# Graph attention kernel: one-hot rows of an edge tile made once for two node tiles, ring of ten, first head's K blocks copied by ScalarE

## What is computed

```python
q = (x @ Wq + bq).reshape(n, H, OUT_DIM); k = ...; v = ...
alpha = jnp.einsum('ehc,ehc->eh', q[dst], k[src]) / np.sqrt(OUT_DIM)
amax = jax.ops.segment_max(alpha, dst, num_segments=n)
ex = jnp.exp(alpha - amax[dst])
denom = jax.ops.segment_sum(ex, dst, num_segments=n)
attn = ex / denom[dst]
agg = jax.ops.segment_sum(attn[:, :, None] * v[src], dst, num_segments=n).reshape(n, HC)
x_attn = agg + x @ Wskip + bskip
h = x_attn @ Wlin + blin + x_attn[:, :OUT_DIM]      # then a layer norm, and x + ...
```

## Time and profile before

| | us |
|---|---|
| median of 3 runs | 1163.88 (1163.66 to 1164.5) |
| the profiled execution, its own time | 1169.78 |
| its span, first to last instruction | 1167.9 |
| TensorE matmuls busy | 1090.4 (93%) |
| VectorE busy | 583.9 (50%) |
| ScalarE busy | 323.4 (28%) |
| GpSimd busy | 125.5 (11%) |

### The profile page before, as it was taken

The page is one execution under the profiler, slowest core; times in us unless marked ns, Lnnn a source line. Parts: engine busy times, 40 slices in busy tenths (PEclk is TensorE's granted clock), DMA queues, the critical chain, the costliest instruction groups (busy, mean ns, idle before and its releaser), DMA issues.

```text
span 1167.9 us, 14839 instructions
## 1 busy us (share of the span) xinstructions
PE 1090.4 (93%) x5666; PEld 892.3 (76%) x5666; DVE 583.9 (50%) x1563; ACT 323.4 (28%) x492; POOL 125.5 (11%) x282
## 2 busy tenths in 40 slices
PE   5789999999999999999999999999999999989871
PEld 4676666668888888888888888888888888868650
DVE  4778888744343343324343332433333245676777
ACT  3443334211232322123232121322322133233210
POOL 1201010100000000000000000000000002535464
PEclk9899999989999999999999999999999999999885
DMA  9426364330010010002000100100010010000111
GB/s 296 177 90 210 122 228 161 120 145 1 1 72 1 1 47 27 2 1 72 1 1 15 58 2 1 73 1 1 1 72 1 1 37 10 18 18 19 36 36 35
DMA packets 14206, 64.42 MB, mean 55 GB/s; under 512 B 1939, under 2 KB 2332, under 8 KB 10553
## 3 DMA queue, kind: packets, MB, share of 16 engines
q1 hardware_dynamic: 9529, 46.67, 11.7%
q0 software_dynamic: 4608, 16.78, 3.7%
HBM read 44.11 MB, written 19.34 MB: 54 GB/s over the span
## 4 chain that ended last, share of the span: by engine, by line
PE 67%; DVE 18%; issue 7%; ACT 4%; POOL 2%; DMA 1%; POOLq 0%; DVEq 0%; SPq 0%; ACTq 0%
PE ps_o L1084 7%; PE ps_o L1086 7%; PE ps_o L1085 7%; PE ps_r L1084 7%; PE ps_r L1086 6%; PE ps_r L1085 6%; PE ps_s L1086 5%; PE ps_s L1085 5%; PE ps_s L1084 5%; PE ps_t L1291 3%; DVE opnd_lo L684 3%; PE ps_t L1084 2%; DVE onehot_src L695 2%; PE ps_t L1086 1%; PE ps_t L1085 1%
## 5 line engine op out<-in xcount | busy, mean ns | idle before, releaser
L1084 PE MATMUL ps_s<-xT_hi,tT 128*128 128x512 f32 (+1 forms) x480 | 176.2, 367 | 2.0 <-DVE top L1041 2.0
L1085 PE MATMUL ps_s<-xT_lo,tT 128*128 128x512 f32 (+1 forms) x480 | 171.2, 357 | 0.0
L1086 PE MATMUL ps_s<-xT_hi,tT 128*128 128x512 f32 (+1 forms) x480 | 171.1, 356 | 0.0
L1084 PE MATMUL ps_o<-y,pT 128*128 128x512 f32 x400 | 158.6, 397 | 0.0
L1086 PE MATMUL ps_o<-y,pT 128*128 128x512 f32 x400 | 157.5, 394 | 0.0
L1085 PE MATMUL ps_o<-y,pT 128*128 128x512 f32 x400 | 157.3, 393 | 0.0
L649 ACT ACTIVATE prob<-prob,nbias 125x1250 f32<-125x1250 f32 x40 | 53.7, 1342 | 259.4 <-DVE nbias L1049 259.4
L1041 DVE CUSTOM_DVE_ANT_0 prob<-ps_s,maskb 125x1250 f32<-125x1250 f32 x40 | 58.2, 1456 | 120.5 <-issue 120.5
L907 DVE TENSOR_TENSOR pT<-ps_t,pT 128x500 fp32r<-128x500 f32 (+1 forms) x120 | 67.3, 589 | 94.0 <-ACT pT L604 94.0
L604 ACT ACTIVATE pT<-ps_t 128x500 fp32r<-128x500 f32 (+1 forms) x120 | 57.9, 518 | 202.2 <-PE ps_t L1291 202.2
L1084 PEld LDWEIGHTS ps_s<-xT_hi,tT 128*128 128x128 f32 (+1 forms) x480 | 90.9, 189 | 18.1 <-DVE top L1041 2.5
(11 more groups left out here) (244 smaller groups left out, 1971.7 us busy)
## 6 DMA issues: line engine op xcount, KB each, us to landing
products<-prod_parts POOLq DMA_DIRECT2D x32, 512.0 KB, 3.2
gbuf<-products SPq DMA_DIRECT2D x4, 2048.0 KB, 7.8
mbuf<-products SPq DMA_DIRECT2D x4, 2048.0 KB, 7.9
stage<-in_Wq SPq DMA_DIRECT2D x4, 1024.0 KB, 7.0
stage<-in_Wk SPq DMA_DIRECT2D x4, 1024.0 KB, 5.2
stage<-in_Wskip SPq DMA_DIRECT2D x4, 1024.0 KB, 5.4
stage<-in_Wv SPq DMA_DIRECT2D x3, 1024.0 KB, 4.8
stage<-in_Wlin SPq DMA_DIRECT2D x3, 1024.0 KB, 4.7
```

The costliest lines, as they stand in the source:

```text
L1084: nc.tensor.matmul(out_, a[0], b[0], start=start, stop=False)
L1085: nc.tensor.matmul(out_, a[0], b[1], start=False, stop=False)
L1086: return nc.tensor.matmul(out_, a[1], b[0], start=False, stop=stop)
```

## The change

Each edge tile's pair of rows is made once, in the product of the first window that holds the tile (`tiles_begun(d)`: 18, then 16 in each, then 14), and used by each window that holds it. The buffer is t modulo 10, and the wait before it is for the last use of tile t - 10. `onehot_dst` is made 250 wide for the 36 tiles that two windows share, and the second window reads columns 125 to 249. VectorE makes the new tiles of a window in quarters of four (`quarter(tiles_begun(p - 1), i)`), TensorE still uses a window in quarters of five. The K blocks of head 0 are copied into `acc` by ScalarE, in its place for block copies, and no longer by VectorE. Three tiles are laid over others to make room (`at_plane`, `spill`, the fallback's row).

```diff
-RING = 9
+RING = 10
-def part(d, i):
-
-    w = window(d)
-    return w[len(w) * i // KC:len(w) * (i + 1) // KC]
+def quarter(some, i):
+
+    return some[len(some) * i // KC:len(some) * (i + 1) // KC]
+def tiles_begun(d):
+
+    return [t for t in window(d) if d == 0 or t not in window(d - 1)]
+def windows_of(t):
+
+    return [d for d in range(NT) if t in window(d)]
+def uses_before(d, t):
+
+    return sum(len(window(e)) for e in range(d)) + len([u for u in window(d) if u < t])
...
-        onehot_dst = [put(f"onehot_dst{i}", [P, R], BF16) for i in range(RING)]
+        onehot_dst = [put(f"onehot_dst{i}", [P, 2 * R], BF16) for i in range(RING)]
...
                 h, kind = divmod(p, 3)
                 if kind == K_PROD:
+                    if h == 0:
+                        act.wait_ge(prod_done, 4 * p + i + 1)
+                        nc.scalar.activation(acc[:, i, :], wbank[i], ACT.Copy).then_inc(prod_free, 1)
...
-            def onehots(d, some):
+            def onehots(some):
                 for t in some:
-                    i = made[0]
-                    if i >= RING:
-                        dve.wait_ge(onehot_used, i - RING + 1)
-                    nc.vector.tensor_scalar(onehot_src[i % RING][0:R, 0:NP], node_id[0:R, 0:NP],
+                    i = t % RING
+                    if t >= RING:
+                        last = windows_of(t - RING)[-1]
+                        dve.wait_ge(onehot_used, uses_before(last, t - RING) + 1)
+                    nc.vector.tensor_scalar(onehot_src[i][0:R, 0:NP], node_id[0:R, 0:NP],
                                             edge_p[0:R, 0, t:t + 1], edge_p[0:R, 1, t:t + 1],
                                             ALU.is_equal, ALU.mult)
-                    nc.vector.tensor_scalar(onehot_dst[i % RING][0:R, :], node_id[0:R, R * d:R * d + R],
-                                            edge_f[0:R, 1, t:t + 1], None, ALU.is_equal).then_inc(onehot_ready, 1)
-                    made[0] += 1
+                    a, w = R * windows_of(t)[0], R * len(windows_of(t))
+                    nc.vector.tensor_scalar(onehot_dst[i][0:R, 0:w], node_id[0:R, a:a + w],
+                                            edge_f[0:R, 1, t:t + 1], None,
+                                            ALU.is_equal).then_inc(onehot_ready, 1)
...
                 for i in some:
+                    if kind == K_PROD and h == 0:
+                        continue
                     dve.wait_ge(prod_done, 4 * p + i + 1)
                     if kind == K_PROD:
                         a = acc[:, i, :]
-                        if h == 0:
-                            ins = nc.vector.tensor_copy(a, wbank[i])
-                        else:
-                            ins = nc.vector.tensor_tensor(a, wbank[i], a, ALU.add)
-                        ins.then_inc(prod_free, 1)
+                        nc.vector.tensor_tensor(a, wbank[i], a, ALU.add).then_inc(prod_free, 1)
...
-                        onehots(p - 1, part(p - 1, i))
+                        onehots(quarter(tiles_begun(p - 1), i))
...
-                for t in part(d, i):
-                    n = used[0]
-                    pe.wait_ge(onehot_ready, n + 1)
-                    nc.tensor.matmul(ps_s[0:R, 0:NP], onehot_dst[n % RING][0:R, :], onehot_src[n % RING][0:R, 0:NP],
-                                     start=(t == window(d)[0]),
+                for t in quarter(window(d), i):
+                    pe.wait_ge(onehot_ready, t + 1)
+                    a = R * windows_of(t).index(d)
+                    nc.tensor.matmul(ps_s[0:R, 0:NP], onehot_dst[t % RING][0:R, a:a + R],
+                                     onehot_src[t % RING][0:R, 0:NP], start=(t == window(d)[0]),
                                      stop=(t == window(d)[-1])).then_inc(onehot_used, 1)
-                    used[0] += 1
```

More of the change, by code:

```diff
@@ L146, in graph_layer @@
         prod = [prod_parts[:, s] for s in range(2)]
-        onehot_src = [put(f"onehot_src{i}", [P, N if i == 0 else NP + 1], BF16) for i in range(RING)]
-        onehot_dst = [put(f"onehot_dst{i}", [P, R], BF16) for i in range(RING)]
+        onehot_src = [put(f"onehot_src{i}", [P, NP + 1], BF16) for i in range(RING)]
+        onehot_dst = [put(f"onehot_dst{i}", [P, 2 * R], BF16) for i in range(RING)]
         node_id = put("node_id", [P, N], F16)
@@ L153, in graph_layer @@
         edge_p = put("edge_p", [P, 2, ET], F32)
-        at_plane = put("at_plane", [P, ET], F32)
         packed = put("packed", [P, NP], I32)
         nibble = [put(f"nibble{i}", [P, NP], I32) for i in range(2)]
-        spill = put("spill", [P, NP], BF16)
         bcol = put("bcol", [P, 4, H * KC], F32)
@@ L170, in graph_layer @@
         weight_i = edge_p[:, 1, :].bitcast(I32)
+        at_plane = edge_i[:, 0, :].bitcast(F32)
+        spill = edge_i[:, 1, :].bitcast(BF16)[:, 0:NP]
+        again_src = stage[1][:].rearrange("p k n -> p (k n)").bitcast(BF16)[:, 0:N]
         uv_rows = stage[0][0:2 * H, 0:2, :]
@@ L178, in graph_layer @@
         vrow_bc = put("vrow_bc", [P, D], F32)
-        assert at[0] <= edge_p_at + 4 * 4 * ET, at[0] - edge_p_at
+        assert at[0] <= edge_p_at + 2 * 4 * ET + 4 * NP, at[0] - edge_p_at
         at[0] = xT_at
@@ L685, in split_lo @@
                                                 ALU.subtract).then_inc(split_ready[odd], 1)
-            made = [0]
-            def onehots(d, some):
+            def onehots(some):
                 for t in some:
-                    i = made[0]
-                    if i >= RING:
-                        dve.wait_ge(onehot_used, i - RING + 1)
-                    nc.vector.tensor_scalar(onehot_src[i % RING][0:R, 0:NP], node_id[0:R, 0:NP],
+                    i = t % RING
[3 more added lines that the diff above has]
+                    nc.vector.tensor_scalar(onehot_src[i][0:R, 0:NP], node_id[0:R, 0:NP],
                                             edge_p[0:R, 0, t:t + 1], edge_p[0:R, 1, t:t + 1],
                                             ALU.is_equal, ALU.mult)
-                    nc.vector.tensor_scalar(onehot_dst[i % RING][0:R, :], node_id[0:R, R * d:R * d + R],
-                                            edge_f[0:R, 1, t:t + 1], None, ALU.is_equal).then_inc(onehot_ready, 1)
-                    made[0] += 1
+                    a, w = R * windows_of(t)[0], R * len(windows_of(t))
+                    nc.vector.tensor_scalar(onehot_dst[i][0:R, 0:w], node_id[0:R, a:a + w],
+                                            edge_f[0:R, 1, t:t + 1], None,
+                                            ALU.is_equal).then_inc(onehot_ready, 1)
             def digits(d):
@@ L856, in rows_again @@
                     def rows_again(t):
-                        nc.vector.tensor_scalar(onehot_src[0][0:R, :], node_id[0:R, :],
+                        nc.vector.tensor_scalar(again_src[0:R, :], node_id[0:R, :],
                                                 edge_f[0:R, 0, bass.ds(t, 1)], None, ALU.is_equal)
-                        nc.vector.tensor_scalar(onehot_dst[0][0:R, :], node_id[0:R, R * d:R * d + R],
+                        nc.vector.tensor_scalar(onehot_dst[0][0:R, 0:R], node_id[0:R, R * d:R * d + R],
                                                 edge_f[0:R, 1, bass.ds(t, 1)], None,
@@ L1158, in cd_by_rows @@
                 ins.then_inc(cd_rows_done, 1)
-            used = [0]
             def count_part(d, i):
@@ L1235, in step @@
                         for c, w in COLS:
-                            ins = nc.tensor.matmul(ps_s[0:R, c:c + w], onehot_dst[0][0:R, :],
-                                                   onehot_src[0][0:R, c:c + w], start=start, stop=stop)
+                            ins = nc.tensor.matmul(ps_s[0:R, c:c + w], onehot_dst[0][0:R, 0:R],
+                                                   again_src[0:R, c:c + w], start=start, stop=stop)
                         ins.then_inc(again_used, 1)
```

## The result

The changed kernel takes 1156.33 us (median of 4 executions, 1155.7 to 1157.36) against 1163.77 before (median of 4, 1162.69 to 1164.5): 7.4 us less, ratio 0.9925 with a 95% interval of 0.9898 to 0.9951. The forecast was 1151.5, in a range of 1145.0 to 1158.5.

The account below looks back on a forecast made before the run. It took TensorE's stalls, waiting on VectorE's chain from block save to one-hot pairs, as the bound. Stage gains of 9.4 us plus 3.0 for clock falls made 12.4, off the median 1163.9: 1151.5 us, range 1145.0 to 1158.5.

Parts of the forecast that it names:

- The chain: Product stages: a third-quarter stall, anchored to the block save before it, ends with the third pair, not the fifth: 0.82 us earlier.
- p = 10: Last product stage: stalled second quarter ends 1.23 us earlier, from a save 0.2 earlier, and last quarter loses 0.4: 1.8 us.
- Width: One-hot rows of the 36 shared tiles, 250 wide instead of 125: 40 ns more each, 130 ns at the other end.
- Weight loads from the second half: TensorE's 36 loads from a shared row's second half: no penalty, 0; at the other end 4.9 us.
- Ring: VectorE's waits for tile t - 10's last use: cost 0, covered by idle time; without cover some 0.3 us a stage.
- K copies of the first head: Stage p = 2: four copies moved from VectorE to ScalarE remove the whole third-quarter stall, 0.74 us.
- The clock: Stages p = 4 and p = 6: both falls from 2.4 to 1.2 GHz behind stalled quarters go, together 2.95 us.
- Falls that stay: Rival, product stages: clock falls stay or others come after remaining short stalls; gain 9.4 us, 1154.5 us; chance 0.20.
- VectorE as the bound: Rival, product stretch: all work VectorE sheds comes off, 15.8 us, 18.8 with the clock: 1145.1 us; chance 0.08.
- Another wait in its place: Rival: VectorE reaches quarter 3 no earlier in use; only p = 2 and the ends gain 1 to 3 us, 1162; chance 0.09.
- slower weight loads: Rival, quarter 1 of p = 2 to 10: second-half loads slower; at 0.34 us each the gain is eaten; chance 0.03.

Follow-up runs that it names:

- the filled one: Kernel before, with ten small matmuls added on TensorE ahead of the edge matmuls of each stalled quarter: median 1163.97 us.
- e1: Changed kernel with the K blocks of the first head copied by VectorE again, one-hot rows still made once: 1155.33 us.
- e2: Kernel before with its 196 pairs and ring of nine, pairs made 6, 7, 2 and 5 in the four places: 1160.49 us.
- e3: Changed kernel with its 16 new tiles made 6, 5, 1 and 4 in the four places instead of 4 each: 1145.31 us.
- e6: Changed kernel with a ring of nine buffers instead of ten: 1155.02 us.
- e9: Changed kernel with new tiles made 6, 5, 1 and 4, and first-head K blocks copied by VectorE again: 1143.77 us.
- e10: Changed kernel with new tiles made 6, 5, 1 and 4 in the four places, run again: 1144.99 us.
- e11: Kernel with shared rows made 6, 5, 1 and 4, plus the first window's first four pairs made ahead of the moments of x: 1143.03 us.

## Why the prediction was right, and where it was off

**The chain.** That a stall ends with the third pair in place of the fifth, that it is anchored to the save before it, and that nothing new comes late in the fourth quarter: right. The stage lengths are the proof. Against the short execution of before, p = 2 to 10 are shorter by 0.72, 0.82, 1.43, 0.91, 0.82, 0.97, 1.10, 0.80 and 1.46 us; the prediction's terms were 0.75, 0.82, 1.4, 0.9, 0.82, 1.0, 1.1, 0.8 and 1.8. Sum 9.0 against 9.4. The one term that missed is p = 10: its second quarter ended 1.26 us earlier in the stage where 1.4 was taken, and its last quarter took 0.54 us where 0.77 had been, 0.23 less for the 0.4 taken.

**The small costs.** Width: 41 ns measured for 40 taken; the other end of its range was 130. By the Trainium skill ("Vector Engine (DVE) Microarchitecture Reference", section 5.1), whose rate the prediction names, 125 columns more were 33 ns (an estimate), and the trace's 41 ns lies near it and far from 130. Weight loads from the second half: 0, as taken. Ring: 0, as taken, shown by the ring of nine. K copies of the first head: the stall of p = 2 went, but the shared rows alone take it away too, so the term was right in size while the cause that it names wasn't needed.

**The clock.** This is the step that failed, and with it the size: 3.0 us for two falls of the clock were taken off the median, on the ground that "the stalls are of the product stretch and I take them as the same in both". The stalls are the same in both kinds of execution; the falls behind them aren't. The 3.0 us in p = 4 and p = 6 were real in the profiled execution and did go. But the short execution that was traced (1162.62) had no fall there to lose. For the four behind the median (1162.69 to 1164.5) this is inferred from their times, which hardly leave room for two falls; one in some of them can't be ruled out. The sign was on the table: the profiled execution lay 5.9 us above a median whose three runs lay within 0.8. A cost that only one execution shows, and which can explain why it is above the others, must not be taken from the median. Without the 3.0 the forecast would have been 1154.5.

**Behind the products.** The stages gained 9.0 us and the medians 7.4. The 1.6 us between are as large as differences that come and go from one execution to the next. From the end of p = 10 to the first pass over scores the same 401 matmuls take one of three times in the fourteen traces, and the clock goes with it: 85.4 to 85.5 us at 1.00 (the short execution of before, the kernel with wasted pairs), 86.9 to 87.0 at 0.98 (both traces of the changed kernel, the filled one, e1, e2, e3 and e6), 88.5 to 88.6 at 0.96 (both long executions of before, e9, e10 and e11). One kernel can show more than one of them: before has 88.5 and 85.4, the kernel with shared and moved rows 87.0 in e3 and 88.5 in e10. In the changed kernel's profile the clock drops behind the thin matmuls which close the products (4 rows wide, 234.75 to 235.7), with matmuls of 0.63 us in place of 0.39; as the short execution of before has the same thin matmuls and no drop, they aren't the whole cause, which stays open. Between the two short executions that were traced, before's of 1162.62 and after's of 1157.36, the account closes: 9.0 us gained in the stages, 1.6 lost in this stretch, 1.2 ahead of p = 2 and 1.0 in the attention loop leave the 5.2 between their spans. Which of these is in the 1.6 us between the medians is not shown.

**The rivals.** Falls that stay: none in p = 3 to 10 in any trace of a kernel with shared rows, so what the rival said of the place was wrong, though its 1154.5 was nearer than the forecast. Its mechanism does live in the kernel whose pairs were only moved: 0.90 in p = 4, behind a second quarter of 2.53 us, 2.1 more than the 0.39 that it takes undisturbed. VectorE as the bound: falls, by the wasted pairs, and by the moved ones, where the same work took 9.8 us less. Another wait in its place and slower weight loads: no trace of either. That the range held the result was luck in part: its upper half stood for falls that stay and for slower weight loads, and what moved the result into it was neither, but the 3.0 us of falls that the traced short execution of before doesn't have.

## What to carry to other kernels

When an engine works in a written order, ask which of its instructions lie between the event that restarts its chain and the signal that the busy engine waits for: only these have a price, and moving them in front of the engine's own idle time can be worth as much as making fewer of them: 9.8 us here on top of the 9.0 of the shared rows. Moved without being shared they gave 2.3 us in p = 3 to 10, less than the shared rows alone gave; p = 5, whose VectorE has little idle time, gained nothing. Before taking a difference off a median, hold the profiled execution's own time against it, and where it lies apart, leave out of the sum what only that execution shows, the slower clock above all. Where the whole stall is already covered, a larger ring or a copy on another engine buys nothing.

## What the runs showed of the hardware

One program on one core took from 1162.4 to 1171.4 us from one execution to the next. In a traced execution of 1169.6 us and one of 1162.6, the stalled quarter of p = 3 is the same (1.93 us each), and VectorE is busy the same 118.2 us in p = 3 to 10. What differs is TensorE's clock. Behind stalls of 2.0 to 2.6 us it falls to its lower level of 1.2 GHz or not: in one execution behind those of p = 4 and 6, in another behind p = 4 and 9, in a third behind none. Each fall costs 1.4 to 1.6 us there. Behind the products the same stretch takes 85.4, 87.0 or 88.5 us at a granted clock of 1.00, 0.98 or 0.96. In the nine traces of kernels with shared rows, whose stalls in p = 3 to 10 are under 1.8 us, no fall came in those stages; the longer group of the kernel with wasted pairs has no trace.
